# The second of three top-k searches: two copies of its numbers in 128 lanes, and eight rounds of four bits in place of twelve of three

## What is computed

```python
input_acts_seq = gelu(einsum('bsd,nd->bsn', x, input_patterns)).mean(axis=1)      # 8 x 2048
top_input_acts, top_input_idx = top_k(input_acts_seq, 256)
input_repr = zeros((8, 2048)).at[brow, top_input_idx].set(top_input_acts)
process_acts = gelu(einsum('bn,pn->bp', input_repr, process_input_weights))        # 8 x 1024
top_process_acts, top_process_idx = top_k(process_acts, 128)                       # the second search
process_weights = softmax(top_process_acts)
aggregated_value = einsum('bk,bkd->bd', process_weights, process_values[top_process_idx])
output_acts_seq = gelu(einsum('bd,od->bo', aggregated_value, output_input_weights)) # 8 x 2048
top_output_acts, top_output_idx = top_k(output_acts_seq, 256)
out_per_seq = einsum('bk,bkm->bm', top_output_acts, output_patterns[top_output_idx])
```

## Time and profile before

| | us |
|---|---|
| median of 3 runs | 596.68 |
| the runs | 594.98, 596.68, 597.45 |
| span of the profiled execution, first to last instruction | 594.4 |

### The profile page before, as it was taken

The page is one execution under the profiler, slowest core; times in us unless marked ns, Lnnn a source line. Parts: engine busy times, 40 slices in busy tenths (PEclk is TensorE's granted clock), DMA queues, the critical chain, the costliest instruction groups (busy, mean ns, idle before and its releaser), DMA issues.

```text
span 594.4 us, 10573 instructions
## 1 busy us (share of the span) xinstructions
PE 433.4 (73%) x3584; PEld 294.6 (50%) x3584; DVE 424.1 (71%) x1719; ACT 273.5 (46%) x657; POOL 81.7 (14%) x233
## 2 busy tenths in 40 slices
PE   2799699742268899578999999999999664602106
PEld 2468586521146555445677776776455553202103
DVE  7644999899946678978888888864444566275673
ACT  3754544732231644345465556654533553253440
POOL 6791000000032253704000000000000000000000
PEclk9998699855559799999999999999999898855556
DMA  9700003288004977310056958600300272000002
GB/s 278 211 1 2 1 1 117 93 148 169 19 1 132 130 144 160 103 40 0 3 80 97 203 81 147 183 1 2 142 0 2 78 276 72 1 0 1 1 1 62
DMA packets 34666, 47.25 MB, mean 79 GB/s; under 512 B 5541, under 2 KB 32054, under 8 KB 32822
## 3 DMA queue, kind: packets, MB, share of 16 engines
q1 hardware_dynamic: 34614, 46.58, 33.2%
HBM read 37.87 MB, written 8.60 MB: 78 GB/s over the span
## 4 chain that ended last, share of the span: by engine, by line
PE 55%; DVE 25%; ACT 10%; issue 5%; POOL 4%; DVEq 0%; POOLq 0%; ACTq 0%
PE ps L2194 8%; PE ps L2148 4%; DVE PR L1049 4%; PE ps L2135 4%; ACT below L1769 4%; PE ps L2124 4%; PE ps L1916 4%; PE ps L2034 4%; PE ps L1924 3%; PE ps L2110 3%; PE ps L2322 2%; PE ps L1980 2%; DVE prod L1045 2%; DVE below L1395 2%; PE ps L1875 2%
## 5 line engine op out<-in xcount | busy, mean ns | idle before, releaser
L1263 DVE TENSOR_REDUCE negm<-ps 112x1 f32<-112x375 f32 x128 | 65.5, 543 | 9.2 <-PE ps L2124 6.0
L1740 ACT ACTIVATE E<-ps 125x448 f32<-125x448 f32 x96 | 52.0, 543 | 43.0 <-PE ps L2135 42.7
L2295 PE MATMUL ps<-cnt,same 128*128 128x3 bf16 (+4 forms) x40 | 6.9, 172 | 61.6 <-ACT below L1769 41.1
L2124 PE MATMUL ps<-ks,qs 96*112 96x375 bf16 x128 | 42.9, 345 | 1.7 <-DVE negm L1263 0.8
L2148 PE MATMUL ps<-E,v 125*32 125x112 f32 x768 | 42.1, 270 | 0.0
L1251 DVE TENSOR_REDUCE acts<-gel 128x4 f32<-128x448 f32 x32 | 19.8, 621 | 29.3 <-ACT gel L1708 29.1
L2135 PE MATMUL ps<-qs,ks 99*125 99x112 bf16 x384 | 39.2, 224 | 1.2 <-DVE qs L1284 0.7
L2135 PEld LDWEIGHTS ps<-qs,ks 99*125 99x125 bf16 x384 | 33.8, 137 | 9.7 <-issue 6.2
L2295 PEld LDWEIGHTS ps<-cnt,same 128*128 128x128 bf16 (+1 forms) x40 | 4.4, 110 | 65.1 <-issue 65.1
L1708 ACT ACTIVATE gel<-ps 128x448 f32<-128x448 f32 x32 | 17.3, 543 | 29.3 <-PE ps L2194 29.3
L789 POOL CAST kp<-kx 128x750 bf16<-128x750 f32 x8 | 7.1, 884 | 165.7 <-ACT path L1623 125.8
(11 more groups left out here) (388 smaller groups left out, 1117.9 us busy)
## 6 DMA issues: line engine op xcount, KB each, us to landing
ks<-key_parts SPq DMA_DIRECT2D x48, 187.5 KB, 7.0
piw<-fn_process_input_weights SPq DMA_DIRECT2D x8, 1024.0 KB, 4.9
key_parts<-kp SPq DMA_DIRECT2D x48, 93.8 KB
ctx_again<-in_ctx SPq DMA_DIRECT2D x7, 512.0 KB
keys<-kx SPq DMA_DIRECT2D x16, 187.5 KB, 2.1
kx<-keys SPq DMA_DIRECT2D x8, 375.0 KB, 6.8
ctxP<-in_ctx SPq DMA_DIRECT2D x8, 256.0 KB, 6.3
patn<-in_L_ffn_input_patterns SPq DMA_DIRECT2D x1, 2048.0 KB, 15.6
```

Source lines behind the costliest of these rows:

```text
L1263: drain(dve.tensor_reduce(negm[:, n:n + 1], bank(nm)[0:S, 0:SC], AX.X, ALU.max, negate=True), nm)
L1740: drain(fn(E[:, (KCH * f + c) % 6, :], bank(nm)[0:KC, 0:4 * S], ACT.Exp), nm)
L2124: fill(mm(bank(nm)[0:S, 0:SC], qs[0:SR, u // 4 % 3, n, :], ks[0:SR, u // 4 % 3, n, :], start=True, stop=True), nm)
```

## The change

Search 1 gets a second copy of its numbers. ACT writes the Gelu twice, side by side, the transpose then fills 128 lanes, and lanes 64 to 127 hold the same numbers as lanes 0 to 63. A round finds four bits with 16 candidates: lanes 0 to 63 count numbers 1 to 8, the other lanes 9 to 16. Eight candidates a lane are shared out as five for DVE and three for ACT. PE makes two products a round, with the two halves of a new matrix `both`, each of which sums the counts of one copy to all 128 lanes; the answer has 16 columns. There are four rounds for each half of the bits, all of them with the full set of candidates; the round with one candidate is left only in search 2. Behind the last round the search goes on in 64 lanes as before. POOL writes `both` and the larger tables `steps` at the place where it wrote `steps` before; they lie in memory that only ACT's early squares used. Two scratch tiles of the search (`kval` and `gt`) share memory with others that are dead by then.

```diff
-STEPS = (tuple(4 ** (7 - r) for r in range(8)),) + ((2 ** 13, 2 ** 10, 2 ** 7, 2 ** 4, 2, 1),) * 2
-NCAND, VC = (3, 7, 7), (3, 4, 4)
+STEPS = (tuple(4 ** (7 - r) for r in range(8)), tuple(16 ** (3 - r) for r in range(4)),
+         (2 ** 13, 2 ** 10, 2 ** 7, 2 ** 4, 2, 1))
+NCAND, VC = (3, 8, 7), (3, 5, 4)
+COPIES = (1, 2, 1)
...
             pool.memset(warm[:, :], 0.0).then_inc(meet_ready, 1)
+            did(pool.memset(both[:, 0, :], 1.0))
...
+            for h in range(4):
+                did(pool.tensor_copy(both[:, h // 2, 64 * (h % 2):64 * (h % 2) + 64], under[0][:, 0:64]))
+            settle()
+            for h in range(2):
+                did(pool.memset(both[64 - 64 * h:128 - 64 * h, h, :], 0.0))
+            settle()
...
-            for k in range(2):
+            for k in range(3):
...
+            for r in range(ROUNDS[1]):
+                for m in range(NCAND[1]):
+                    did(pool.memset(steps[1][64:128, r, m:m + 1],
+                                    float((m + 1 + NCAND[1]) * STEPS[1][r]) - (0.5 if m >= VC[1] else 0.0)))
...
-            def largest(k, lanes, keep):
+            def largest(k, numbers, keep):
+                one = B * numbers // 128
+                lanes = COPIES[k] * one
+                columns = COPIES[k] * NCAND[k]
...
-                did(dve.memset(most[0:lanes, 0:VC[k]], numbers - keep + 0.5))
-                if VC[k] < NCAND[k]:
-                    did(dve.memset(most[0:lanes, VC[k]:NCAND[k]], numbers - 2 * keep + 0.5))
+                for at in range(0, columns, NCAND[k]):
+                    did(dve.memset(most[0:lanes, at:at + VC[k]], numbers - keep + 0.5))
+                    if VC[k] < NCAND[k]:
+                        did(dve.memset(most[0:lanes, at + VC[k]:at + NCAND[k]], numbers - 2 * keep + 0.5))
...
-                    only = last and k > 0
+                    only = last and k == 2
...
-                    tests = 1 if only else NCAND[k]
+                    tests = 1 if only else columns
...
+                lanes = one
+                val = kval[0:lanes, :]
+                v = {n: t[0:lanes, :] for n, t in tiles.items()}
...
             def signs(k, r):
-                if r % ROUNDS[k] == ROUNDS[k] - 1:
+                if k == 2 and r % ROUNDS[k] == ROUNDS[k] - 1:
                     return
-                n = B * (NIT, NPT, NOT)[k]
+                n = COPIES[k] * B * (NIT, NPT, NOT)[k]
...
-            fn(acts[1][:, :], praw[:, :], ACT.Gelu).then_inc(acts_ready, 1)
+            fn(acts[1][:, :].rearrange("p (h e) -> p h e", h=2), praw[:, :].unsqueeze(1).broadcast_to([128, 2, B * NPT]),
+               ACT.Gelu).then_inc(acts_ready, 1)
...
-                if k:
+                if k == 1:
+                    pe.wait_ge(signs_ready, r + 1)
+                    for h in range(2):
+                        ins = mm(bank(nm)[:, m * h:m * h + m], both[:, h, :], cnt[:, 0:m], start=True, stop=True)
+                    fill(ins, nm)
+                    return
```

More of the change, by code:

```diff
@@ L249, in build_program @@
         onesb = ra.take("onesb", [128, SC], BF16)
-        steps = [ra.take(f"steps{k}", [128, ROUNDS[k], NCAND[k]]) for k in range(2)]
         iota_i = ra.take("iota_i", [128, 1], I32)
@@ L293, in build_program @@
         sx = ra.take("sx", [S, B])
+        tables = Region(ra.at)
         actscr = ra.take("actscr", [128, D])
+        steps = [tables.take(f"steps{k}", [128, ROUNDS[k], NCAND[k]]) for k in range(3)]
+        both = tables.take("both", [128, 2, 128], BF16)
+        assert tables.at <= ra.at
         rw = Region(ra.at)
@@ L410, in build_program @@
         oiwT = r1.take("oiwT", [128, NO])
-        acts = [acts0] + [r1.take(f"acts{k + 1}", [128, B * n]) for k, n in enumerate((NPT, NOT))]
+        acts = [acts0] + [r1.take(f"acts{k + 1}", [128, 128]) for k in range(2)]
         aT = r1.take("aT", [128, 128])
+        kval = Region(r1.at).take("kval", [128, 128])
         key = r1.take("key", [128, 128], I32)
+        gt = Region(r1.at).take("gt", [128, 128])
         sgn = r1.take("sgn", [128, 128], I32)
@@ L423, in build_program @@
         cnt = r1.take("cnt", [128, 8], BF16)
-        reached = r1.take("reached", [128, max(NCAND)])
+        reached = r1.take("reached", [128, 2 * max(NCAND)])
         nsel = r1.take("nsel", [128, 1])
@@ L764, in _ @@
             pool.memset(warm[:, :], 0.0).then_inc(meet_ready, 1)
+            did(pool.memset(both[:, 0, :], 1.0))
+            settle()
+            groups = both[:, 0, :].rearrange("p (g j) -> p g j", j=NPT)
+            did(pool.affine_select(out=groups, in_=groups, compare_op=ALU.is_ge, fill=0.0, base=0,
+                                   pattern=[[-NPT, 128 // NPT], [0, NPT]], channel_multiplier=1))
+            settle()
+            did(pool.affine_select(out=groups, in_=groups, compare_op=ALU.is_ge, fill=0.0, base=NPT - 1,
+                                   pattern=[[NPT, 128 // NPT], [0, NPT]], channel_multiplier=-1))
+            settle()
+            did(pool.tensor_tensor(under[0][:, 0:64], both[:, 0, 0:64], both[:, 0, 64:128], ALU.add))
+            settle()
+            for h in range(4):
+                did(pool.tensor_copy(both[:, h // 2, 64 * (h % 2):64 * (h % 2) + 64], under[0][:, 0:64]))
+            settle()
+            for h in range(2):
+                did(pool.memset(both[64 - 64 * h:128 - 64 * h, h, :], 0.0))
+            settle()
             quarter = 4 * B
@@ L1348, in largest @@
                 bits = aT[0:lanes, :].bitcast(I32)
[L1349 to L1352, removed]
+                tiles = {"key": key, "sgn": sgn, "low": eq, "khi": khi, "klo": klo, "kval": kval, "cand": cand,
+                         "nextb": nextb, "nsel": nsel, "bound": bound, "eq": eq, "gt": gt, "need": need,
+                         "incl": incl, "sel": sel}
+                v = {n: t[0:lanes, :] for n, t in tiles.items()}
                 for n in ("cand", "nextb"):
@@ L1401, in largest @@
                         settle()
-                        did(ts(v["nextb"], steps[min(k, 1)][0:lanes, q + 1, :], v["bound"], None, ALU.add))
+                        did(ts(v["nextb"], steps[k][0:lanes, q + 1, :], v["bound"], None, ALU.add))
                     nm = ("count", k, r)
                     wait_filled(dve, nm)
-                    tests = 1 if only else NCAND[k]
+                    tests = 1 if only else columns
                     drain(stt(reached[0:lanes, 0:tests], bank(nm)[0:lanes, 0:tests], 1.0, most[0:lanes, 0:tests],
```

22 lines of the change are left out of this document (11 added, 11 removed).

## The result

The changed kernel takes 588.3 us (median of 4 runs, 584.89 to 589.76), against 597.07 us for the kernel before on the same chip: ratio 0.9866, 95% interval 0.983 to 0.9902. Two more sets of the same kernel on other chips gave 589.14 us (0.9866, 0.984 to 0.9892) and 589.73 us (0.9915, 0.9882 to 0.9947); all 15 runs together have their median at 589.18. So the change is faster, as forecast, by 5.9 to 8.8 us in the medians, or 5.1 to 8.0 by the ratios, where the forecast had 5.2; the intervals of the first two sets leave 5.2 us out, that of the third takes it in.

The account below looks back on a forecast made before the run. Search 1 was taken as a bare chain of round trips that bounds the kernel. Its 5.33 us saving less 0.15 us added gave 5.2 us net: 596.68 - 5.2 = 591.5 us, range 589.7 to 593.5.

Parts of the forecast that it names:

- The round: Search 1: a round with five DVE counts, built from two rounds that DVE paced, takes 2.25 us instead of 2.09.
- The sum and the way in: Search 1 falls from 24.31 to 18.98 us, 5.33 less; steps from Gelu to first count add 0.15 us.
- The second load: PE's second load and product in each round of search 1 add only 0.03 us.
- the 592.3 us: Time if PE's loads grew with columns, as the skill says: 0.107 us more a round, 0.9 us in eight.
- POOL at nothing: POOL's larger tables and `both`, some 5 us of work, cost nothing because POOL waits 125.75 us behind them.
- The products didn't run one behind the other: Rival on PE in search 1: second product waits for the first, 0.26 us a round; 593.3 us, chance 0.09.
- the waits did count: Rival in search 1: only instructions count, not waits; 594.4 us, within no change, chance 0.04.
- DVE's counts still follow at 0.27 us: Rival in search 1: counts get dearer with DVE and ACT on 128 lanes, 0.45 us each; 598.7 us, chance 0.02.
- What comes later starts earlier: Behind search 1: later work starts earlier, with no DMA under way to hold it back; no further gain or cost.
- PE's clock is no term: Search 1's stretch: PE's clock stays at the 1.2 GHz level and two small products a round leave PE idle; no cost.

Follow-up runs that it names:

- c1: The kernel before with only POOL's new tables, `both` and the new places in memory; 596.56 us, ratio 1.0014 to before.
- e2: The kernel before with 6 chained DVE additions ahead of search 1; 595.34 us, ratio 0.9997 to before.
- b1: The changed kernel with 16 chained DVE additions ahead of the first candidates of search 1; 596.56 us, ratio 0.9997 to before.
- d1: The kernel before with one full round less in each half of search 1, threshold coarser; 589.5 us, ratio 0.9876 to before.
- i3: The kernel before with dense unread PE products from round 10 of search 2 on; 591.9 us, ratio 0.9943 to before.
- e1: The changed kernel with 6 chained DVE additions ahead of search 1; 592.92 us, ratio 0.9948 to before.
- g1: A second profile of the kernel of e1, nothing changed; 593.88 us in one run.

## Why the prediction was right and wrong

*The round*: right. It takes 2.25 us, and each of its parts came as forecast: 0.26 to 0.28 us from count to count, 0.23 us for PE's pair, 0.49 us from comparison to the next count. It was built from two other rounds in which DVE set the pace, with the same chain and other numbers of counts.

*The sum and the way in*: right. The search took 18.92 us where 18.98 were forecast, and the way in 0.19 us more where 0.15 were. The search gained 5.4 us, 5.2 net, as forecast.

*The second load*: right, no cost beyond the pair's 0.03 us. Both loads of a round show 0.14 us together. By the section LDWEIGHTS of the Trainium skill's "TensorE: Matmul & The Clock Gate", which lets a load's time grow with its columns, two of 128 columns would be an estimated 0.21 us; the trace goes on disagreeing with it, and the 592.3 us by it didn't come.

*POOL at nothing*: right. Its tables took the time out of its wait, 120.17 us instead of 125.75, and c1 shows no effect.

*The rivals*: none came. The products didn't run one behind the other (0.23 us), the waits did count, and DVE's counts still follow at 0.27 us with ACT's beside them in all 128 lanes.

*Behind the search*: here it failed. "What comes later starts earlier" took the end as a block that is moved whole, 10.4 us wherever it starts, and "PE's clock is no term" was argued for the stretch of the rounds alone. But the end holds 48 products that the end of the program waits for, and their time depends on when the clock returns. The missing term is -2.4 us (10.4 to 8.0); with it the forecast is 596.68 - 5.2 - 2.4 = 589.1 us, below the range's lower bound of 589.7, and the gain 7.6 us, beside measured gains of 8.8, 7.0 and 5.9 us in the three sets. That it came out as a gain is a matter of the place: e2 got a short end by moving the last products later. What the first four runs lie below that (588.3) is within the scatter from search 0 and ahead of it. The prediction foresaw that something behind the search might take gain back, not that it might add some. The trace of before had the sign: in one row of eight like steps on `x`, the pace changed from 0.86 us to 0.5 as the granted clock rose from 0.50. A range that took this term in would have reached 589.1 us before any scatter.

## What to carry to other kernels

Cost a change by its own chain, and then ask of everything behind it whether its duration depends on when it runs: where a stretch of TensorE's work sits on the path and a window shows the granted clock changing inside it, its time is a term with two ends, not a constant. When a gain is larger than its mechanism explains, delay the changed kernel by the gain, and shorten the old one by other means; the two together tell whether the surplus belongs to the edit or to the place in time (b1 and d1). And an experiment that should remove a cause has to be read for whether it did: four runs with added products left the clock low where it mattered, and only the denser ones tested the theory.

## What the runs showed of the hardware

The same 32 products took 3.64 us at the 1.2 GHz level and 1.93 us at 2.4 GHz (before and i3). The 16 behind them took 3.68 us at 2.4 GHz (after, i3) and 6.07 us where the clock rose only inside them (before). At the lower level PE set the pace of DVE's last steps (0.86 us each, before), at the higher DVE itself did (3.50 us for eight, after).

Work that nobody reads paid for itself: 3.7 us in the medians in i3. A program with six additions more on its critical path could be as fast as without them (e2), and one program showed two ends, 8.2 and 10.0 us (e1, g1).
